# Transformer stage: the values product issued in two halves, its result taken one head-step later, and ScalarE's exponentials put ahead of the turned rows

## What is computed

```
x = _ln(src) * (1.0 + scale) + shift
q, k, v = x @ Wq + bq, x @ Wk + bk, x @ Wv + bv      # 16 heads of 16
scores = einsum('bhqd,bhkd->bhqk', q / 4, k) + attention_bias
scores = where(src_mask, -inf, scores)
ctx = softmax(scores) @ v
x = x + (ctx @ Wo + bo)
h = _ln(x) * g2 + beta2
out = x + (_gelu2(h @ W1 + b1) @ W2 + b2)
```

## Time and profile before

| what | before |
|---|---|
| median of three runs | 1372.82 us |
| the profiled execution's own time | 1370.21 us |
| its span, first to last instruction | 1368.4 us |
| mean granted TensorE clock | 0.978 of full speed |
| PE busy, share of the span | 1237.3 us, 90% |
| DVE busy | 974.0 us, 71% |
| ACT busy | 901.0 us, 66% |
| POOL busy | 702.8 us, 51% |
| DMA, mean rate | 148 GB/s |

### The profile page before, as it was taken

One profiled execution on the slowest core, in us unless ns is written; L12 is line 12 of the kernel. 1 busy time (PEld: TensorE's weight loads), 2 busy tenths in 40 slices (PEclk: granted clock), 3 DMA queues, 4 the chain that ended last, 5 costly groups with the idle time before them and its releaser, 6 DMA issues.

```text
span 1368.4 us, 34309 instructions
## 1 busy us (share of the span) xinstructions
PE 1237.3 (90%) x9799; PEld 1141.1 (83%) x9799; DVE 974.0 (71%) x2767; ACT 901.0 (66%) x2319; POOL 702.8 (51%) x612
## 2 busy tenths in 40 slices
PE   4887599999999999994579999999999999999996
PEld 3776599999999999993458888888888888888885
DVE  5676687988788888763478677676666766777662
ACT  3343577787787778771357777677677767777772
POOL 2677386877787777774324433434333343333322
PEclk9999999999999999996799999999999999999998
DMA  5785311212111221213877666667666676656620
GB/s 182 241 271 193 115 51 49 58 58 58 59 58 45 53 60 56 59 43 106 270 225 220 198 213 200 213 204 229 196 209 188 212 228 196 210 184 211 216 86 16
DMA packets 184660, 203.13 MB, mean 148 GB/s; under 512 B 18209, under 2 KB 172657, under 8 KB 184529
## 3 DMA queue, kind: packets, MB, share of 16 engines
q1 hardware_dynamic: 169232, 161.65, 38.3%
q10 hardware_dynamic: 9120, 23.33, 5.4%
q0 software_dynamic: 6176, 16.79, 3.7%
HBM read 160.01 MB, written 41.71 MB: 147 GB/s over the span
## 4 chain that ended last, share of the span: by engine, by line
PE 42%; issue 4%; ACT 3%; DVE 3%; DMA 1%; ACTq 1%; POOL 0%; another core or an unknown queue 0%; POOLq 0%; DVEq 0%
PE ps_p L1384 8%; PE ps_s L1370 4%; PE ps_ctx L1400 4%; PE ps_s L1372 4%; PE ps_out L1496 3%; PE ps_q L1496 3%; PE ps_q L1482 2%; PE ps_k L1482 2%; PE ps_q L1449 2%; PE ps_out L1440 2%; ACT bias L1278 2%; PE ps_q L1457 2%; PE ps_k L1449 2%; PE ps_q L1486 1%; PE ps_k L1486 1%
## 5 line engine op out<-in xcount | busy, mean ns | idle before, releaser
L1278 ACT ACTIVATE bias<-bias,neg_max 128x256 f32<-128x256 f32 x512 | 255.1, 501 | 85.2 <-DVE neg_max L1606 83.2
L348 POOL TENSOR_TENSOR w_lo<-w,w_hi 128x512 fp32r<-128x512 f32 x156 | 242.1, 1572 | 0.0
L1606 DVE CUSTOM_DVE_ANT_0 bias<-ps_s,bias 128x256 f32<-128x256 f32 x512 | 194.4, 417 | 35.5 <-PE ps_s L1372 19.3
L751 DVE TENSOR_TENSOR w_lo<-w,w_hi 128x512 fp32r<-128x512 f32 x156 | 150.9, 1006 | 68.1 <-ACT w_hi L429 66.4
L550 PE MATMUL ps_y<-w_hi,hidT_hi 128*128 128x256 f32 x624 | 180.2, 289 | 1.9 <-DVE token_rows L765 1.9
L537 PE MATMUL ps_h<-htokT_hi,w_hi 128*128 128x256 f32 x624 | 178.3, 286 | 3.2 <-DVE htokT_lo L756 3.2
L1384 PE MATMUL ps_p<-const,bias 128*128 128x128 f32 x1024 | 156.9, 276 | 23.7 <-ACT bias L1278 22.3
L537 PE MATMUL ps_h<-htokT_lo,w_hi 128*128 128x256 f32 x624 | 178.0, 285 | 0.0
L537 PE MATMUL ps_h<-htokT_hi,w_lo 128*128 128x256 f32 x624 | 178.0, 285 | 0.0
L550 PE MATMUL ps_y<-w_hi,hidT_lo 128*128 128x256 f32 x624 | 177.0, 284 | 0.0
L550 PE MATMUL ps_y<-w_lo,hidT_hi 128*128 128x256 f32 x624 | 177.0, 284 | 0.0
(11 more groups left out here) (281 smaller groups left out, 3521.3 us busy)
## 6 DMA issues: line engine op xcount, KB each, us to landing
bias<-bias_dram SPq DMA_DIRECT2D x128, 512.0 KB, 4.8
w<-w_dram ACTq DMA_DIRECT2D x32, 512.0 KB
xin<-dispatch SPq DMA_DIRECT2D x39, 256.0 KB, 2.9
expert_out<-token_rows SPq DMA_DIRECT2D x39, 256.0 KB, 2.2
q_stack<-q_hi_rows SPq DMA_DIRECT2D x64, 128.0 KB, 2.9
q_stack<-q_lo_rows SPq DMA_DIRECT2D x64, 128.0 KB, 3.0
k_stack<-k_hi_rows SPq DMA_DIRECT2D x60, 128.0 KB, 2.9
k_stack<-k_lo_rows SPq DMA_DIRECT2D x60, 128.0 KB, 2.9
```

The costliest lines, as they stand in the source:

```text
L348: pool.tensor_tensor(w2_part["lo"][:, k, :], w2_piece(e, k), w2_part["hi"][:, k, :].bitcast(F32), ALU.subtract).then_inc(sem("w2_split"), 1)
L751: dve.tensor_tensor(w1_part["lo"][:, k, :], w1_piece(e, k), w1_part["hi"][:, k, :].bitcast(F32), ALU.subtract).then_inc(sem("w1_split"), 1)
L1278: act.activation(head_rows(h, j), head_rows(h, j), ACT.Exp, scale=-1.0, bias=neg_max[par][:, h, j:j + 1], accum_out=total[par][:, h, j:j + ...
L1606: dve.tensor_tensor_reduce(head_rows(h, j), ps_s[h % 2][:, j * T:(j + 1) * T], head_rows(h, j), -1.0, LARGEST, ALU.add, ALU.min, neg_max[p ...
```

## The change

The values product is split by blocks of 128 tokens: PE issues the first block at head-step 4 and the second at head-step 5. Each block raises the semaphore `v_done` by one, so those who wait for it now count two per entry. DVE takes the values at head-step 6 instead of 5, behind the minimum of head 7, and `split_hT` stands behind it (in the one step where there is no next entry, `split_hT` stands where it was). On ACT the exponentials of head 7 stand ahead of `take_hT`. No instruction's size or operands change.

```
 ACT modulate
-            wait_free(act, sem("v_done"), n)
+            wait_free(act, sem("v_done"), J * n)
 ACT step
+                if exists(ahead):
+                    exponentials(ahead, head, par if head else 1 - par)
                 if h == 6 and exists(n - 1):
                     take_hT(n - 1)
-                if exists(ahead):
-                    exponentials(ahead, head, par if head else 1 - par)
 PE
-        def values(n):
-            pe.wait_ge(sem("q_split"), 2 * C * (n + 1))
-            for kt in range(J):
-                for c in range(C):
-                    last = pe.matmul(ps_q[:, kt * D:(kt + 1) * D], xmT[:, c, kt * P:(kt + 1) * P], wv[:, c, :],
-                                     start=(c == 0), stop=(c == C - 1))
+        def values(n, kt):
+            if kt == 0:
+                pe.wait_ge(sem("q_split"), 2 * C * (n + 1))
+            for c in range(C):
+                last = pe.matmul(ps_q[:, kt * D:(kt + 1) * D], xmT[:, c, kt * P:(kt + 1) * P], wv[:, c, :],
+                                 start=(c == 0), stop=(c == C - 1))
             last.then_inc(sem("v_done"), 1)
 PE step
-                    if h == 4:
-                        values(n + 1)
+                    if 4 <= h < 6:
+                        values(n + 1, h - 4)
 DVE take_values
-            dve.wait_ge(sem("v_done"), n + 1)
+            dve.wait_ge(sem("v_done"), J * (n + 1))
 DVE step
-                    if h == 6:
+                    if h == 6 and not exists(n + 1):
                         split_hT(n - 1)
...
-                    if h == 5:
-                        if isinstance(n, int) and n == -1:
-                            dve.wait_ge(sem("v_zeroed"), 2)
-                        take_values(n + 1, 1 - par)
+                if exists(n + 1) and h == 6:
+                    if isinstance(n, int) and n == -1:
+                        dve.wait_ge(sem("v_zeroed"), 2)
+                    take_values(n + 1, 1 - par)
+                    if exists(n - 1):
+                        split_hT(n - 1)
```

## The result

The kernel before took 1372.32 us (median, 1371.41 to 1374.18), the changed one 1363.59 us (1363.02 to 1364.10), a ratio of 0.9927 with a 95% interval of 0.991 to 0.9943. The time fell by 8.7 us where 12.0 were forecast. The profiled execution took 1363.64 us with a span of 1361.8 us, against 1370.21 and 1368.4 before.

A forecast was written before the change was run, and what follows sets the result against it. PE's own work bounds the kernel (busy 526.6 of 546 us), plus small waits, chiefly for ACT's exponentials. Gain 0.80 us in each of 15 entries, other terms nothing: 1372.8 - 12.0 = 1360.8 us; range 1356.6 to 1367.

The forecast's parts named there:

- The wait of head-step 7: PE's turn_probs waits for ACT's exponentials, mostly 1.27 us shown, in 15 steps; claimed to go completely, with 0.45 us to spare.
- the new wait of head 8: PE in head-step 8 would wait 0.62 us for ACT's exponentials, shown as about 0.5 us.
- The term 0.80 x 15 = 12.0 us: Net gain over head-steps 7 and 8, taken as 0.80 us for each of 15 entries.
- the last entry: Same sum at head 8 in the last of the 15 entries: a gain of 0.74 us.
- everything comes back: Rival: head 8's exponentials ready in time, so all 1.43 us gained 15 times, 21.5 us: 1351.3 us; chance 0.05.
- slower: Rival: head 7's minimum late, so ACT's exponentials delay take_hT; 4.4 us lost, 1377.2 us; chance 0.06.
- The joint of the values: Rival: values products before weigh must run out, costing 0.35 us in 16 entries: 1366.4 us; chance 0.08; forecast took nothing.
- DVE's idle time before L1677: Idle time ahead of split_hT on DVE, claimed to fall from 1.5 to about 0.8 us at no cost.
- the change has nothing for them but trifles: PE's waits outside head-step 7, in entry 0 and scattered, were claimed to give next to nothing.
- entry 0 does not move: No turned row in entry 0, so the values' move changes nothing for PE that could be priced.
- the tail stays: After 1330 us there are no exponentials and no values product, so that stretch was claimed unchanged.
- a late bias load: Rival: bias for head 14 lands too late for DVE, at worst taking the whole gain, 1372.8 us; chance 0.07.

The follow-up runs named there:

- experiment 2: Changed kernel with ACT's order put back, leaving only the values product in two halves and take_values a step later: 1372.09 us, ratio 0.9994.
- experiment 3: Changed kernel with POOL's four indirect gather transfers issued for entry 0 only: 1357.51 us, ratio 0.9892.
- experiment 4: Kernel before the change with POOL's four indirect gather transfers issued for entry 0 only: 1370.16 us, ratio 0.9978.
- experiment 5: Changed kernel with ACT's take_ctx of the second group moved behind the exponentials of head 3 in head-step 2: 1358.22 us, ratio 0.9881.
- the repeat: The changed kernel run and profiled once more, nothing altered: 1362.88 us, ratio 0.9927.
- experiment 1: Kernel before the change with only ACT's exponentials of head 7 put ahead of take_hT: 1361.24 us, ratio 0.9923.
- experiment 10: Changed kernel with take_ctx behind head 3's exponentials, turn_h first in head-step 6, and each step's first bias load one head later: 1356.17 us, ratio 0.9871.
- experiment 7: Changed kernel with POOL's four indirect transfers replaced by plain ones of the same size: 1354.58 us, ratio 0.9854.

## Why the prediction was right, and where it was off

**The wait of head-step 7** is gone in all 15 steps, and head-steps 6 and 7 take 4.34 us together instead of 5.16. The prediction had the new wait of head 8 at 0.62 us; measured by distance it is 2.99 - 2.38 = 0.61 us. As shown it is 0.18, not 0.5. The term 0.80 x 15 = 12.0 us is 12.03 in the changed kernel's trace and 12.13 without the gather. Only the last entry is off: it gains 0.61 us where 0.74 were forecast. The rivals "everything comes back" and "slower" fall: `take_hT` starts 0.63 us after the first row of `turn_h` (0.64 before), and ACT still waits for it.

**The joint of the values** costs nothing. The first half leaves 0.86 us of head-step 4 and brings 0.86 to head-step 5, not 0.77 each way, and their sum changes by 0.04 us over 15 entries. PE's rows, answering to the earlier trace rows:

```profile
1014.96 0.60 PE L1384 MATMUL ps_p<-const,bias 128*128 128x128 f32 x4
...
1016.74 0.60 PE L1384 MATMUL ps_p<-const,bias 128*128 128x128 f32 x4
1017.17 1.03 PE L1457 MATMUL ps_q<-wv,xmT 128*128 128x256 f32 x4
1018.13 1.07 PE L1400 MATMUL ps_ctx<-probT,v_pad 128*32 128x256 f32 x16
```

The Trainium skill's rule that changing the tiling mode drains TensorE (TensorEngine Tiling (Array Packing), Key Properties) adds nothing here: products in front of the change cost no more than transposes did, and experiment 2 has a ratio of 0.9994. Whether the drain is paid both times is not shown.

**DVE's idle time before L1677** did not fall from 1.5 to 0.8 us; it is 1.60. That was an error of counting: the minimum and the values both stood ahead of that gap before, and they still do. It had no consequence, since I took no cost from it.

**The step that failed** is what the prediction put at nothing outside head-steps 7 and 8: that the waits elsewhere are scattered and "the change has nothing for them but trifles", that entry 0 does not move, and that the tail stays. The sum is 3.3 us off (8.7 instead of 12.0). Profile against profile, the body is 7.28 us shorter, the stretch behind it 3.0 us longer and the one in front of it 2.3 us shorter, 6.6 us in all; the other 2.1 us of the 8.7 are that the profile of the kernel before lies that far below its median. That the time fell inside the range is partly luck: the upper part of the range stood for the joint of the values, which costs nothing, and not for what was lost. The terms that were not in the sum:
- head 2 to head 3, +3.86 us: `take_ctx`, held by PE's late updates beside the gather, stood ahead of the exponentials of head 3 with no slack at all (2.64 us is what PE needs). I had put the other waits down as scattered. Experiments 3, 4 and 5 show it, with 5.4 us back for one move on ACT. Some of this is chance of the execution. Of the entries 3, 4, 6, 8, 10 and 12, all six have the long distance in the changed kernel and five in its repeat, three each in experiments 1 and 2, and one in the profile before. Why it comes so much more often in the changed kernel is not shown, and with one profile each for most kernels it may be partly chance.
- a late bias load in entry 4, +0.71 us, which the prediction's range had. It is absent in the repeat, and experiment 10 shows how near the bound it is.
- entry 0, -1.88 us, which I had priced at nothing ("the move changes nothing for PE that I can price"). Experiment 2 has -1.75 with the values alone, so it is theirs.
- the start of the entries, h0-2, +1.21 us (0.79 in the repeat, 0.98 without the gather), 0.3 of it in entry 1, where PE's product for q waits 0.51 us for `modulate`, and 0.6 in entry 5, where only 0.12 us of it is this wait and the rest is not explained; and +0.6 us over head-steps 8 to 12, since head 8 to head 9 takes 2.37 to 2.40 instead of 2.34 us in every entry. Both come again in the repeat and without the gather, so they belong to the change; they were not forecast.
- behind the last `turn_probs`, +3.0 us: 34.3 us instead of 31.4.

The last one goes with the clock. The windows of this stretch in the kernel before (columns as in the earlier trace rows):

```profile
1342.00:1348.00 6.00, 2.05 (x16) 1.86 (x16) 2.93 (x9) 0.00 (x0) 0.71 (x1) 0.89 0.00 0
1348.00:1354.00 6.00, 5.15 (x25) 4.76 (x26) 1.24 (x3) 1.19 (x2) 1.27 (x1) 0.54 0.00 0
```

And of the changed kernel:

```profile
1332.00:1338.00 6.00, 4.29 (x24) 3.48 (x16) 1.08 (x2) 0.38 (x1) 0.00 (x0) 0.55 0.00 0
1338.00:1344.00 6.00, 2.13 (x8) 1.73 (x9) 2.89 (x9) 0.60 (x1) 1.98 (x2) 0.74 0.00 0
1344.00:1350.00 6.00, 6.00 (x36) 5.80 (x36) 1.38 (x2) 2.26 (x4) 1.30 (x1) 0.69 0.00 0
```

The mean granted clock is 0.54 in one window before, and 0.55, 0.74 and 0.69 in three after: the lower level of 1.2 GHz in one stretch before and in two after, behind stretches in which PE was partly idle (2.05 us busy of 6 in the first row of the kernel before; waits of 0.50, 0.50 and 1.28 us ahead of 1334 us in the changed one). The repeat has 33.0 us there, and the other kernels 31.4 to 34.3, in no order that follows their edits. It goes with the clock instead: the stretch takes 31.4 us in the three profiles with some 7 us at the lower level, 32.9 to 33.4 in the four with some 10 us, and 33.1 to 34.3 in the five with 14 or 17 us. So "the tail stays" holds for its work and not for its time, within some 3 us.

The first setup-and-route part also varies (the first `turn_probs` comes at 672.1 us before, 669.8 after, and anywhere from 667.3 to 672.4 in the others). Together with the clock at the end this can make single profiles differ from the medians by a microsecond or two. The mean granted clock of the whole profile, 0.932 against 0.978 before, is no sign of a slower part: from 37 to 153 us the changed kernel's trace has the lower level and that of the kernel before the full clock, yet the transposes of L489 start 0.21 us apart there in both. The same two kinds of execution, near 0.934 and near 0.976, are found among the runs of the kernel before.

## What to carry to other kernels

When one wait goes, add up the start-to-start distances of every stage, not only of the one that was edited: a stage without slack elsewhere can take back a third of the gain. An instruction that waits for a late result must not stand in an in-order engine ahead of work whose input is ready; moving it behind that work gave 12 us at `take_hT` and 5 us at `take_ctx`. Where a wait moves on to the next stage, ask which instruction starts its chain, and move that one: `turn_h` half a microsecond earlier gave 6.5 us more.

## What the runs showed of the hardware

- Beside POOL's indirect transfers (L1206), PE's semaphore updates are held back and then come together: ACT, a consumer of PE, starts 3.42 us after its producer's first product instead of 1.14 us. PE itself works on, and ACT's updates in the same time are not held (34 of 36 on record within 0.06 us, PE's 54 all late). With plain transfers of the same size it is 1.14 us (experiment 7). The stop does not show as anybody's busy time: the sign is a wait released by "remote".
- Beside them PE's update comes 1.2 to 2.8 us after the product starts instead of 0.42, and the same kernel shows an early and a late one in the same entry in two executions (entry 4: 3.37 and 2.65 us from head 2 to head 3). What chooses is open; landings of the bias load are not needed for the late one (experiment 10).
- Beside the indirect transfers the trace lacks part of the updates (248 of 257 of `turn_probs`, 485 of 513 of `minimum`), and has all of them without a gather or with the plain one. That no update is recorded does not say that none was made.
- PE's idle time as shown (0.18 us) can be a third of what is lost by start-to-start distance (0.61 us): the product ahead is drawn 0.28 us long where starts are 0.12 us apart.
- The clock fell to half once or twice in the kernel's last 30 us, behind stretches in which PE was idle in part (a last fall, less than 4 us before the end, not counted). The stretch behind the last `turn_probs`, the same work in all, took 31.4 us with some 7 us of it at the lower level and 32.9 to 34.3 us with 10 us or more.
